# Weight and key preparation of three attentions as steps of the first batch, new step orders, and feed-forward scaling on VectorE

## The chip, the cores and the metric

The program runs on one core of one Trainium2 chip. The metric is the device time of one execution in microseconds (us). In the text PE is TensorE, DVE is VectorE, ACT is ScalarE, POOL is GpSimd and SP is SyncE, which here only issues DMAs. Each runs its own instruction stream in order; they meet through counting semaphores.

## The reference

Four layers work in turn on x (8 batches x 256 tokens x 128 features, fp32). Each layer is a gated cross-attention to a context (8 x 64 x 128) and a gated feed-forward:

```
x = x + tanh(g_xattn[l]) * attention_l(layernorm(x), ctx)
x = x + tanh(g_ffn[l])   * ffn_l(layernorm(x))          # l = 0..3
```

- Attention 0: 16 heads of 8 features; q = x Wq + bq; k, v = ctx Wkv + bkv; softmax; out Wo + bo.
- Attention 1: keys and values of the context and of x itself, no biases in q and k, a tanh gate in place of the first key's weight, and a layer norm of the result before the last projection.
- Attention 2: as attention 0 with a mask (8 x 1 x 256 x 64) that is scaled and added to the scores; scores divided by sqrt(128).
- Attention 3: 8 heads of 64 features.
- Feed-forward 0: 16 experts of 32 features, the best 4 of each token; 1: 8 experts of 352, the best 2; 2: one gated network of 384; 3: 8 experts of 64, the best 2 by groups, and a shared one.

## The kernel before

`build` (L2216) calls `setup`, then for each layer `attention` (L212; the last layer has `attention3`, L904) and `ffn` (L1234) or, for layers 0 and 3, `ffn_wide` (L1754). Nothing of two stages overlaps except some statistics. x stays in SBUF the whole time.

**A step table sets the order in an attention.** `STEPS_0` to `STEPS_3` list steps as (name, batch offset, group...). `passes(eng, does)` walks for v = -2 to 10 over the table, and for each row issues on engine `eng` that engine's part of the step, for batch v + offset. So all five engines have the same order of steps, each with its own part of them, and a row's place in the table decides what stands ahead of it on every engine. One walk over the table is one batch, here called a **cycle**.

A batch goes: "scale" (DVE L804, layer norm's scaling, with POOL in `turn` adding the gated output bias to x), "turn" (PE transposes L518, ACT and DVE split into a high and a low part, L686 and L810), "proj" (PE L535 to L537, ACT L698, DVE L823: q of one of 4 groups of 4 heads), "keys" (POOL L398 spreads the context's keys by head), "scores" (PE L551, in attention 2 also L553 with the mask, and DVE L835 takes row maxima), "maxima" (PE transposes L571, ACT, DVE L860), "weights" (PE scores again, transposed, less the maximum, ACT L711 exp), "pv" (PE L624), then the output is turned, divided, projected and added to x (`y`, DVE, semaphore x_done). In attention 2 "mask_in" (POOL L453) and "mask" (PE L526, ACT L692, DVE L817) prepare a batch's mask. `attention3` has steps of its own with the same walk.

**The prologue** of `attention` comes whole ahead of the table. DVE: 16 bn_aggr (L749); in layers 0 and 2 a wait for all of the layer's DMAs (`loaded`, in layer 2 also for the mask), then two copies of a bias row spread by head (L754, L756); the two weights split into high and low parts with spread columns, `wx` (L769, L770); PE turns the bias row into columns with 8 matmuls of one row (L481; the trace counts 16, each in two passes), DVE takes them (L773 to L775). PE: four key sums of three matmuls (L488 to L490), one for each group, into four PSUM banks; ACT L671 and DVE L785 take each in turn, through the one tile `hk`. PE: two value sums (L494, L496), ACT L674 takes them. DVE L792 copies a constant. POOL sets `mx`, `kc`, `vc` (L365 to L367), and scales `bo` (L385). Every engine's part ends with a wait for all of that, so that no PE instruction of batch 0 comes before it; DVE scales batch 0 (L804) only after its own last prologue instruction.

**`ffn_wide`**: four groups of 512 tokens. For each: statistics (DVE L2065, L2070), rstd (POOL L1895, L1897), scaling (group 0 on DVE, L2094; groups 1 to 3 on POOL, L1906), PE transposes (L1942), router logits (L1951). After the fourth, DVE routes all tokens at once (some 8 us up to `gx`, L2152), and PE spreads the gates (L1962). Meanwhile PE computes up-projections (L1972 to L1974, "up"): in layer 0 it has N = 16 of them ahead of the first gates. The scratch `gx` is zeroed by DVE (L2076) after the first group's statistics.

Of the kernel before, what the change touches and what calls it, by code (L numbers as in the profile page):

```python
# [113 lines left out]
def setup(pr):  # L114
# [60 lines left out]
    ("values", 0), ("scale", 1), ("scores", 0, 2, 0), ("proj", 0, 3), ("keys", 0, 3), ("maxima", 0, 1), ("weights", 0, 0, 0), ("pv", -1, 1, 0),  # L175
    ("turn", 1), ("scores", 0, 3, 0), ("proj", 1, 0), ("keys", 1, 0), ("maxima", 0, 2), ("weights", 0, 1, 0), ("spread", 0), ("o_turn", -1),
    ("o_norm", -1), ("scores", 1, 0, 0), ("proj", 1, 1), ("keys", 1, 1), ("maxima", 0, 3), ("weights", 0, 2, 0), ("pv", 0, 0, 0), ("o_scale", -1),
    ("on_turn", -1), ("scores", 1, 1, 0), ("proj", 1, 2), ("keys", 1, 2), ("maxima", 1, 0), ("weights", 0, 3, 0), ("y", -1),
# [3 lines left out]
    ("y", -2), ("weights", -1, 3, 3), ("keys", 0, 2), ("keys", 0, 3), ("weights", -1, 3, 4), ("scores", 0, 1, 4), ("scores", 0, 2, 0), ("scale", 1),  # L182
    ("proj", 0, 3), ("values", 0), ("maxima", 0, 1), ("pv", -1, 1, 0), ("weights", 0, 0, 0), ("pv", -1, 1, 1), ("keys", 1, 0), ("scores", 0, 2, 1),
    ("scores", 0, 2, 2), ("weights", 0, 0, 1), ("weights", 0, 0, 2), ("pv", -1, 1, 2), ("weights", 0, 0, 3), ("scores", 0, 2, 3),
    ("weights", 0, 0, 4), ("scores", 0, 2, 4), ("turn", 1), ("weights", 0, 1, 0), ("scores", 0, 3, 0), ("scores", 0, 3, 1), ("maxima", 0, 2),
    ("proj", 1, 0), ("spread", 0), ("pv", -1, 1, 3), ("pv", -1, 1, 4), ("scores", 0, 3, 2), ("weights", 0, 1, 1), ("weights", 0, 1, 2),
    ("scores", 0, 3, 3), ("scores", 0, 3, 4), ("o_turn", -1), ("weights", 0, 1, 3), ("weights", 0, 1, 4), ("o_norm", -1), ("scores", 1, 0, 0),
    ("proj", 1, 1), ("weights", 0, 2, 0), ("pv", 0, 0, 0), ("weights", 0, 2, 1), ("weights", 0, 2, 2), ("scores", 1, 0, 1), ("scores", 1, 0, 2),
    ("maxima", 0, 3), ("pv", 0, 0, 1), ("pv", 0, 0, 2), ("weights", 0, 2, 3), ("scores", 1, 0, 3), ("o_scale", -1), ("weights", 0, 2, 4),
# [2101 lines left out]
```

## Time and profile before

| | us |
|---|---|
| three runs | 1176.37, 1176.54, 1165.46 (median 1176.37) |
| profiled execution | 1168.41, its span 1166.6 |
| attention 0, 16.86 to 126.20 | 109.34 |
| feed-forward 0, to 193.60 | 67.40 |
| attention 1, to 442.70 | 249.10 |
| feed-forward 1, to 722.40 | 279.70 |
| attention 2, to 862.40 | 140.00 |
| feed-forward 2, to 922.60 | 60.20 |
| attention 3, to 1070.20 | 147.60 |
| feed-forward 3, to 1166.60 | 96.40 |

The stages' bounds are the first instruction of each stage in the timeline. The profiled execution spends 1.8 us outside its span. Busy shares of the whole span are 78% PE, 64% DVE, 48% ACT and 37% POOL; the mean granted clock of PE is 0.889 of full speed. A cycle is measured between the ends of `y` (x_done) of two batches.

### The profile page before, as it was taken

How to read it: one execution, taken by the hardware profiler on the slowest of the kernel's cores; microseconds unless marked ns; L12 is line 12 of the kernel's file. 1: busy time of each engine (PE TensorE's matmuls, PEld its weight loads, DVE VectorE, ACT ScalarE, POOL GpSimd, SP SyncE). 2: the span in 40 equal slices, each digit the busy share in tenths (PEclk: the TensorE clock that was granted, in tenths of full speed). 3: DMA queues.
4: the chain of work that ended last, by engine and by line, in shares of the span. 5: the costliest groups of instructions: out<-in, count | busy, mean ns of one | idle time of the engine just before them, and what ended most of it. 6: DMA issues, size and time to landing. Idle time of an engine off the chain costs nothing. (4 is left out here: it accounts for less than half of the span.)

```text
span 1166.6 us, 17099 instructions
## 1 busy us (share of the span) xinstructions
PE 912.0 (78%) x5366; PEld 686.6 (59%) x5366; DVE 746.8 (64%) x1823; ACT 563.8 (48%) x1091; POOL 428.7 (37%) x575
## 2 busy tenths in 40 slices
PE   2799586689899885888888885688858588885696
PEld 2677464556565643666666663477745357884574
DVE  3688467579998865757666564467756414555576
ACT  0477253367776762545555543256634233331364
POOL 2333414133443323655656565233310132220434
PEclk9799688689998995999999998689979769998699
DMA  4000000000001000000000001000000200000001
GB/s 129 1 2 2 1 0 22 1 20 20 19 21 37 20 2 0 1 1 1 1 1 1 1 1 23 16 2 1 2 21 1 72 1 1 1 1 1 0 1 37
DMA packets 25606, 14.12 MB, mean 12 GB/s; under 512 B 10775, under 2 KB 25006, under 8 KB 25390
## 3 DMA queue, kind: packets, MB, share of 16 engines
q1 hardware_dynamic: 25518, 13.03, 4.2%
q8 instruction: 45, 0.74, 0.3%
q14 instruction: 43, 0.35, 0.1%
HBM read 11.98 MB, written 1.05 MB: 11 GB/s over the span
## 5 line engine op out<-in xcount | busy, mean ns | idle before, releaser
L1433 POOL TENSOR_TENSOR L1f_h<-L1f_h,L1f_gb 128x512 f32<-128x512 f32 (+1 forms) x96 | 152.2, 1589 | 105.5 <-DVE L1f_h L1726 97.3
L711 ACT ACTIVATE L_pt<-bank 128x512 f32<-128x512 f32 x224 | 127.1, 597 | 44.0 <-PE bank L597 35.0
L398 POOL TENSOR_TENSOR L_kc<-L_kc_all,const 128x256 fp32r<-128x256 f32 x96 | 59.1, 618 | 177.8 <-PE bank L597 114.1
L698 ACT ACTIVATE L_part<-bank,L_bias_ca,const 128x256 fp32r<-128x256 f32 x128 | 68.9, 563 | 89.3 <-PE bank L537 88.8
L1562 ACT ACTIVATE L1f_a<-bank 128x512 f32<-128x512 f32 (+1 forms) x96 | 57.3, 597 | 112.7 <-PE bank L1487 112.6
L1726 DVE TENSOR_TENSOR L1f_h<-L1f_a,bank 128x512 f32<-128x512 f32 (+1 forms) x96 | 65.5, 682 | 70.8 <-ACT L1f_a L1562 70.3
L1734 DVE TENSOR_TENSOR L1f_h_lo<-L1f_h,L1f_h_hi 128x512 fp32r<-128x512 f32 (+1 forms) x96 | 88.2, 919 | 11.1 <-ACT L1f_h_hi L1575 11.1
L837 DVE TENSOR_REDUCE L_ms<-bank 128x2 f32<-128x512 f32 x128 | 84.0, 686 | 7.3 <-PE bank L558 7.2
L835 DVE TENSOR_REDUCE L_mc<-bank 128x8 f32<-128x512 f32 (+1 forms) x96 | 65.4, 682 | 19.5 <-PE bank L553 12.2
L1485 PE MATMUL bank<-L1f_xt_hi,big_hi 128*128 128x512 f32 (+1 forms) x192 | 77.8, 405 | 0.0
L1486 PE MATMUL bank<-L1f_xt_lo,big_hi 128*128 128x512 f32 (+1 forms) x192 | 76.8, 400 | 0.0
L1487 PE MATMUL bank<-L1f_xt_hi,big_lo 128*128 128x512 f32 (+1 forms) x192 | 76.7, 400 | 0.0
L558 PE MATMUL bank<-L_k,L_q 32*128 32x256 f32 x256 | 54.3, 335 | 16.6 <-DVE L_ms L837 15.1
L551 PE MATMUL bank<-L_kc,L_q 128*128 128x256 f32 x192 | 54.1, 345 | 15.8 <-DVE L_msk L817 6.4
L1507 PE MATMUL bank<-L1f_h_hi,big_hi 128*128 128x512 f32 (+1 forms) x96 | 41.4, 431 | 30.0 <-DVE L1f_h_lo L1734 29.7
L823 DVE SCALAR_TENSOR_TENSOR L_q<-bank,L_bias_c,L_part 128x256 fp32r<-128x256 f32 x96 | 46.2, 482 | 25.8 <-ACT L_part L698 23.6
L1575 ACT CAST L1f_h_hi<-L1f_h 128x512 fp32r<-128x512 f32 (+1 forms) x96 | 59.0, 615 | 2.1 <-POOL L1f_h L1433 2.1
L558 PEld LDWEIGHTS bank<-L_k,L_q 32*128 32x128 f32 x256 | 35.5, 199 | 32.9 <-DVE L_ms L837 21.3
L535 PE MATMUL bank<-L_xt_hi,L_wx 128*128 128x256 f32 x128 | 43.1, 337 | 9.9 <-DVE L_xt_lo L810 9.9
L551 PEld LDWEIGHTS bank<-L_kc,L_q 128*128 128x128 f32 x192 | 34.5, 208 | 27.6 <-issue 16.5
L705 ACT ACTIVATE L_hm<-bank,const 128x256 fp32r<-128x256 f32 x96 | 45.1, 470 | 6.3 <-PE bank L571 6.1
L1507 PEld LDWEIGHTS bank<-L1f_h_hi,big_hi 128*128 128x128 f32 (+1 forms) x96 | 17.9, 187 | 49.9 <-DVE L1f_h_lo L1734 44.8
(412 smaller groups left out, 2570.2 us busy)
## 6 DMA issues: line engine op xcount, KB each, us to landing
L_raw<-in_L_ffn_w_dram SPq DMA_DIRECT2D x8, 176.0 KB, 2.3
L_raw<-in_L_ffn_v_dram SPq DMA_DIRECT2D x8, 176.0 KB, 2.4
const<-in_const_dram SPq DMA_DIRECT2D x1, 1036.0 KB, 5.1
x<-in_x_dram SPq DMA_DIRECT2D x2, 512.0 KB
L_raw<-in_L_ffn_w_dram SPq DMA_DIRECT2D x8, 128.0 KB, 2.5
L_mask<-in_mask_Bx1xSxS_ff_dram SPq DMA_DIRECT2D x2, 512.0 KB
out_dram<-x SPq DMA_DIRECT2D x2, 512.0 KB
L_raw<-in_L_ffn_w_dram SPq DMA_DIRECT2D x8, 48.0 KB, 2.6
```

What stands on the lines that cost most here:

```text
L551: last = pe.matmul(o[:, t * S:(t + 1) * S], q[:, g, ts], kc[:, g], start=True, stop=not masked)
L558: last = pe.matmul(o[:, t * S:(t + 1) * S], q[rows, g, t * P:(t + 1) * P], k[rows, g], start=True, stop=True)
L698: last = act.activation(part[:, i].bitcast(F32R), b_proj[:, i * S:(i + 1) * S], ACT.Identity, bias=bias_ca[:, i, g:g + 1], scale=pr.c("ak" ...
L711: act.activation(pt[:, g // 2, (g % 2) * NS + (HEADS_1[i] if own_keys else i)], b_st[(g * NS + i) % 2][:], ACT.Exp, scale=scale).then_inc( ...
L835: dve.tensor_reduce(mc[:].rearrange("p t j -> p (t j)"), by_head[:, :, start:], AX_X, ALU.max).then_inc(sem["sc_taken"], 1)
L837: dve.tensor_reduce(ms[:, :, i - 1], bank.rearrange("p (t s) -> p t s", s=S), AX_X, ALU.max).then_inc(sem["sc_taken"], 1)
L1433: pool.tensor_tensor(h[0:m, r], h[0:m, r], gb[0:m, gate_slot(c)], ALU.mult).then_inc(sem["h_done"], 1)
L1485: pe.matmul(bank[0:m], hi[:, at:at + m], xh, start=True, stop=False)
L1486: pe.matmul(bank[0:m], hi[:, at:at + m], xl, start=False, stop=False)
L1487: last = pe.matmul(bank[0:m], lo[:, at:at + m], xh, start=False, stop=True)
L1726: dve.tensor_tensor(h[0:m, r], a[0:m, r], b_u[c % NS][0:m], ALU.mult).then_inc(sem["half_done"], 1)
L1734: dve.tensor_tensor(h_lo[0:m, r], h[0:m, r], h_hi[0:m, r].bitcast(F32), ALU.subtract).then_inc(sem["lo_done"], 1)
```

## The change

1. The prologue of `attention` becomes steps (`p_moments`, `p_bias`, `p_bias_c`, `p_wx`, `p_zero`, `p_kc`, `p_bo`, `p_const`, `p_vc`, and in layer 1 `p_wf`, `p_wx_zero`, `p_gate`, `p_vg`). A second table for each layer, `FIRST_0` to `FIRST_2`, orders them together with steps of batch 0; `passes` walks it once, ahead of the other table, and leaves those steps out later. The counting semaphores of the prologue and `loaded` are replaced by one for each thing that is waited for: the keys of group g wait for that group's sum, batch 0's values for the value sums, and so on. The key sums now use two banks in turn and the value sums one, since the others hold batch 0's work.
2. `p_moments 0` takes the two tiles of batch 0, `p_moments 1` the other 14, later.
3. The q and k biases come as rows of `bias_t` by 8 small DMAs, already spread, and one PE transpose makes them columns; the two copies and the 8 one-row matmuls go.
4. The mask of attention 2 gets its tile ahead of feed-forward 1, whose SP issues its two DMAs and waits for them.
5. All four step tables are new.
6. In `ffn_wide` DVE scales all four groups, POOL zeroes `gx` after the logits' first steps, the statistics come one group earlier in the order, and in layer 0 11 up-projections instead of 16 stand ahead of the gates.

```diff
 STEPS_2 = (
-    ("values", 0), ("scale", 1), ("mask_in", 1), ("scores", 0, 2, 0), ("proj", 0, 3), ("keys", 0, 3), ("maxima", 0, 1), ("weights", 0, 0, 0),
...
+    ("spread", 0), ("turn", 1), ("o_scale", -2), ("weights", 0, 0, 0), ("scores", 0, 3, 0), ("maxima", 0, 2), ("proj", 1, 0), ("o_norm", -1),
...
+FIRST_2 = (
+    ("p_bias",), ("p_const",), ("p_moments", 0), ("p_wx", 1), ("p_bias_c",), ("p_zero",), ("mask_in", 0), ("p_wx", 0), ("p_kc", 0), ("scale", 0),
+    ("mask", 0), ("keys", 0, 0), ("p_bo",), ("turn", 0), ("p_kc", 1), ("keys", 0, 1), ("proj", 0, 0), ("p_moments", 1), ("p_kc", 2), ("p_kc", 3),
+    ("scores", 0, 0, 0), ("proj", 0, 1), ("p_vc", 0), ("keys", 0, 2), ("keys", 0, 3), ("scores", 0, 1, 0), ("maxima", 0, 0), ("p_vc", 1),
+    ("proj", 0, 2),
+)
...
         def passes(eng, does):
+            for step, *at in first:
+                if step in does:
+                    does[step](*at)
             for v in range(-2, B + 3):
                 for step, db, *at in table:
-                    if step in does and 0 <= v + db < B:
+                    if step in does and 0 <= v + db < B and (step, v + db, *at) not in first:
                         does[step](v + db, *at)
...
+                    for i, (name, row) in enumerate({0: (("L0_xattn_bq", 0), ("L0_xattn_bkv", 0)), 2: (("L2_xattn_bq", 0), ("L2_xattn_bk", 0))}[layer]):
+                        for t in range(4):
+                            sp.dma_start(bias_t[NG * i:NG * i + NG].rearrange("g (h t d) -> g h t d", h=GH, t=4)[:, :, t],
+                                         ins[name][0:D].rearrange("(g h d) -> g h d", g=NG, h=GH)).then_inc(sem["bias_dma"], 16)
...
+                def p_bias():
+                    if biased:
+                        pe.wait_ge(sem["bias_dma"], 16 * 8)
+                        pe.transpose(b_sc[1][:, 0:2 * NG], bias_t[:], pr.id(2 * NG)).then_inc(sem["bias_turned"], 1)
...
+                def p_kc(g):
+                    if g == 0:
+                        pe.wait_ge(sem["wx_ready"], 2)
+                    need(pe, sem["kc_split"], g - 1)
                     cols = slice(g * P, (g + 1) * P)
+                    bank = b_st[g % 2]
...
                 def keys(b, g):
                     need(pool, sem["st_done"], b * U + (g + 1) * NS - U)
+                    if b == 0:
+                        pool.wait_ge(sem["kc_split"], g + 1)
...
-        AHEAD = N if layer == 0 else 6
-        first = [("moments", 0), ("scale", 0), ("moments", 1), ("turn", 0), ("scale", 1), ("logits", 0), ("moments", 2), ("turn", 1), ("scale", 2),
-                 ("up", 0), ("logits", 1), ("moments", 3), ("turn", 2), ("scale", 3), ("up", 1), ("logits", 2), ("turn", 3), ("logits", 3),
-                 ("route", 0)] + [("up", n) for n in range(2, AHEAD)]
+        AHEAD = 11 if layer == 0 else 6
+        first = [("moments", 0), ("prepare", 0), ("moments", 1), ("scale", 0), ("moments", 2), ("scale", 1), ("turn", 0), ("logits", 0), ("moments", 3),
+                 ("turn", 1), ("zero", 0), ("scale", 2), ("up", 0), ("logits", 1), ("turn", 2), ("scale", 3), ("up", 1), ("logits", 2),
+                 ("turn", 3), ("logits", 3), ("route", 0)] + [("up", n) for n in range(2, AHEAD)]
...
                 def scale(i):
-                    if i:
-                        return
-                    dve.wait_ge(sem["rstd"], 1)
+                    dve.wait_ge(sem["rstd"], i + 1)
+                    need(dve, sem["xn_turned"], i - 1)
```

**The start of attention 2 on PE, before.** Names: `ctx_hi`, `ctx_lo` the context's parts, `wx` the weights' parts, `xn` the scaled x, `mk` a mask tile.

```order
L481 MATMUL bank<-L_ones,L_bias_x 128x1 x8
L488 MATMUL bank<-ctx_hi,L_wx 128x512
L489 MATMUL bank<-ctx_lo,L_wx 128x512
L490 MATMUL bank<-ctx_hi,L_wx 128x512
...
L494 MATMUL bank<-L_bias_row,L_ones 128x512
L496 MATMUL bank<-w_att,ctx_t 128x128 x4
L494 MATMUL bank<-L_bias_row,L_ones 128x512
L496 MATMUL bank<-w_att,ctx_t 128x128 x4
L518 MATMUL bank<-const,L_xn 128x128 x2
L535 MATMUL bank<-L_xt_hi,L_wx 128x256
L536 MATMUL bank<-L_xt_lo,L_wx 128x256
L537 MATMUL bank<-L_xt_hi,L_wx 128x256
```

And now (lines 516 to 518 are the key sums, 551 the transposes of x, 570 to 572 the projection, 588 and 590 the scores):

```order
L508 MATMUL bank<-const,L_bias_t 128x8
L516 MATMUL bank<-ctx_hi,L_wx 128x512
L517 MATMUL bank<-ctx_lo,L_wx 128x512
L518 MATMUL bank<-ctx_hi,L_wx 128x512
L559 MATMUL bank<-const,L_mk 128x128 x2
L551 MATMUL bank<-const,L_xn 128x128 x2
L516 MATMUL bank<-ctx_hi,L_wx 128x512
L517 MATMUL bank<-ctx_lo,L_wx 128x512
L518 MATMUL bank<-ctx_hi,L_wx 128x512
L570 MATMUL bank<-L_xt_hi,L_wx 128x256
L571 MATMUL bank<-L_xt_lo,L_wx 128x256
L572 MATMUL bank<-L_xt_hi,L_wx 128x256
```

The turn and the first projection of batch 0 stood behind all four key sums and both value sums; now they stand behind two key sums, and the value sums (L526, L530) behind the first scores.

**A steady cycle of attention 2 on PE, before**, from the second half of one batch's "weights" (L588, L590, L591) on:

```order
L588 MATMUL bank<-L_q,L_kc 128x256
L590 MATMUL bank<-L_msk_all,L_i 128x256
L591 MATMUL bank<-L_mt,L_selc 128x256
L526 MATMUL bank<-const,L_mk 128x128 x2
L641 MATMUL bank<-const,L_ot 128x128 x4
L551 MATMUL bank<-L_kc,L_q 128x256
L553 MATMUL bank<-L_i,L_msk 128x256
```

And now ("weights" are L628, L630, L631):

```order
L683 MATMUL bank<-const,L_ot 128x128 x4
L559 MATMUL bank<-const,L_mk 128x128 x2
L570 MATMUL bank<-L_xt_hi,L_wx 128x256
L571 MATMUL bank<-L_xt_lo,L_wx 128x256
L572 MATMUL bank<-L_xt_hi,L_wx 128x256
L628 MATMUL bank<-L_q,L_kc 128x256
L630 MATMUL bank<-L_msk_all,L_i 128x256
L631 MATMUL bank<-L_mt,L_selc 128x256
L628 MATMUL bank<-L_q,L_kc 128x256
L630 MATMUL bank<-L_msk_all,L_i 128x256
L631 MATMUL bank<-L_mt,L_selc 128x256
L588 MATMUL bank<-L_kc,L_q 128x256
```

Between the mask's transposes and the next batch's first scores, which need the mask through ACT and DVE, stood one operation of four transposes; now a projection and a whole "weights" step stand there.

**The start of feed-forward 3 on DVE, before** (`mv` the statistics, `xt_lo` the low part of the transposed tile):

```order
L2065 BN_STATS st<-x 128x6 x4
L2070 BN_AGGR L3f_mv<-st 128x2 x4
L2076 MEMSET L3f_gx 128x2048
...
L2094 TENSOR_SCALAR L3f_xn<-x,L3f_mv,L3f_rstd 128x128 x4
L2065 BN_STATS st<-x 128x6 x4
L2070 BN_AGGR L3f_mv<-st 128x2 x4
L2099 TENSOR_TENSOR L3f_xt_lo<-bank,L3f_xt_hi 128x512
```

And now:

```order
L2117 BN_STATS st<-x 128x6 x4
L2122 BN_AGGR L3f_mv<-st 128x2 x4
L2143 TENSOR_SCALAR L3f_xn<-x,L3f_mv,L3f_rstd 128x128 x4
L2117 BN_STATS st<-x 128x6 x4
L2122 BN_AGGR L3f_mv<-st 128x2 x4
L2143 TENSOR_SCALAR L3f_xn<-x,L3f_mv,L3f_rstd 128x128 x4
L2148 TENSOR_TENSOR L3f_xt_lo<-bank,L3f_xt_hi 128x512
```

The zeroing of `gx` is gone from DVE, and the second group is scaled there before the first group's transposed tile is split.

## Rows read from the trace of the kernel before

**Rows 1.** The page, busy time, its share of the span, and instructions.
```profile
PE 912.0 (78%) x5366; PEld 686.6 (59%) x5366; DVE 746.8 (64%) x1823; ACT 563.8 (48%) x1091; POOL 428.7 (37%) x575
```

**Rows 2.** Windows, attentions 0 to 3: us; busy per engine; PE clock, DMA.
```profile
16.86:126.20 109.34, 90.40 (x624) 70.77 (x624) 77.36 (x207) 60.21 (x134) 39.67 (x68) 0.92 0.03 7
193.60:442.70 249.10, 209.13 (x1712) 141.29 (x1712) 199.85 (x455) 155.28 (x314) 86.11 (x183) 0.89 0.07 19
722.40:862.40 140.00, 106.44 (x768) 87.58 (x768) 81.86 (x217) 68.75 (x143) 41.65 (x80) 0.85 0.05 9
922.60:1070.20 147.60, 119.72 (x664) 98.70 (x664) 58.17 (x117) 44.44 (x85) 37.97 (x64) 0.89 0.06 15
```

**Rows 3.** Timeline, prologue of attention 0: start, us, instruction, [idle before <- releaser].
```profile
17.78 0.36 SPq L331 DMA_DIRECT2D L_bo<-in_L_xattn_bo_dram  x1
21.12 0.41 DVE L754 COPY L_bias_x<-L_bias_row 1x512 f32<-1x512 f32 x1 [2.93 <-DMA L_bo<-in_L_xattn_bo_dram]
22.35 3.57 PE L481 MATMUL bank<-L_ones,L_bias_x 1*128 1x1 f32 x16 [14.57 <-DVE L_bias_x L756]
26.79 0.79 PE L488 MATMUL bank<-ctx_hi,L_wx 128*128 128x512 f32 x1 [0.86 <-DVE L_bias_ca L775]
34.53 0.75 DVE L785 SCALAR_TENSOR_TENSOR L_kc_all<-bank,L_bias_c,L_q 128x512 fp32r<-128x512 f32 x1 [0.97 <-ACT L_q L671]
34.74 1.16 PE L496 MATMUL bank<-w_att,ctx_t 128*128 128x128 f32 x8
40.13 0.80 PE L551 MATMUL bank<-L_kc,L_q 128*128 128x256 f32 x2 [1.18 <-DVE L_q L823]
```

**Rows 4.** Timeline, start of attention 2.
```profile
732.41 0.41 DVE L754 COPY L_bias_x<-L_bias_row 1x512 f32<-1x512 f32 x1 [7.88 <-DMA L_mask<-in_mask_Bx1xSxS_ff_dram]
752.60 0.55 PE L551 MATMUL bank<-L_kc,L_q 128*128 128x256 f32 x1 [1.17 <-DVE L_msk L817]
```

**Rows 5.** Timeline, the first reduction of attention 1.
```profile
216.42 0.68 DVE L835 TENSOR_REDUCE L_mc<-bank 128x8 f32<-128x504 f32 x1 [0.89 <-PE bank L551]
```

**Rows 6.** Windows, single cycles: attentions 0, 2, 3, 1; then the first of attention 2.
```profile
86.23:95.75 9.52, 8.89 (x74) 7.02 (x73) 8.31 (x23) 6.84 (x16) 3.67 (x7) 1.00 0.00 0
811.65:824.22 12.57, 10.78 (x93) 9.08 (x92) 8.99 (x25) 7.89 (x17) 4.43 (x9) 1.00 0.01 1
1021.97:1035.77 13.80, 12.28 (x82) 10.92 (x81) 6.88 (x12) 4.47 (x9) 3.35 (x7) 1.00 0.00 0
281.65:307.13 25.48, 22.70 (x210) 14.96 (x211) 24.31 (x55) 18.65 (x38) 9.86 (x21) 1.00 0.08 22
758.84:773.50 14.66, 12.58 (x73) 11.03 (x74) 8.01 (x22) 8.26 (x16) 4.15 (x9) 0.69 0.00 1
```

**Rows 7.** Waits in attention 2, 765 to 848: us in total, times, longest.
```profile
PE bank L551 <- DVE L_msk L817: 5.2, 7, 1.1
PE bank L526 <- DVE L_mt L860: 4.0, 6, 0.7
```

**Rows 8.** Waits in attention 3, 985 to 1065: us in total, times, longest.
```profile
PE bank L1073 <- ACT L_rb L1157: 3.9, 6, 0.7
```

**Rows 9.** Timeline, start of feed-forward 0.
```profile
128.98 1.76 DVE L2076 MEMSET L0f_gx<- 128x2048 f32 x1 [0.38 <-issue]
139.26 1.11 PE L1942 MATMUL bank<-const,L0f_xn 128*128 128x128 f32 x4 [2.18 <-POOL L0f_xn L1906]
145.10 3.13 POOL L1906 TENSOR_SCALAR L0f_xn<-x,L0f_mv,L0f_rstd 128x128 f32<-128x128 f32 x4
160.68 0.69 DVE L2152 TENSOR_TENSOR L0f_gx<-L0f_p,L0f_total 128x512 f32<-128x512 f32 x1
163.89 0.60 PE L1962 MATMUL bank<-const,L0f_gx 128*128 128x128 f32 x4
```

**Rows 10.** Lines, POOL's `kc` memset and DVE's scaling in attentions: ns min/median/max.
```profile
L366 POOL MEMSET L_kc<- x3: 952/952/1562, 22.0 to 728.1; 128x1024 f32 x3
L804 DVE TENSOR_SCALAR L_xn<-x,L_mv,L_rstd x48: 334/340/504, 35.6 to 837.1; 128x128 f32<-128x128 f32 x48
```

More of the change, by code:

```diff
@@ L174 @@
 STEPS_0 = (
[L175 to L178, printed above, removed]
+    ("keys", 0, 0), ("o_scale", -2), ("weights", -1, 3, 0), ("scores", 0, 2, 0), ("turn", 1), ("maxima", 0, 1), ("weights", 0, 0, 0),
@@ L179 @@
 )
 STEPS_1 = (
[L182 to L189, printed above, removed]
@@ L190 @@
-    ("scores", 1, 0, 4), ("proj", 1, 2), ("keys", 1, 1), ("on_turn", -1), ("scores", 1, 1, 0), ("maxima", 1, 0), ("weights", 0, 3, 0),
-    ("pv", 0, 0, 3), ("pv", 0, 0, 4), ("scores", 1, 1, 1), ("weights", 0, 3, 1), ("weights", 0, 3, 2), ("scores", 1, 1, 2), ("scores", 1, 1, 3),
+    ("y", -2), ("weights", -1, 3, 3), ("weights", -1, 3, 4), ("scores", 0, 1, 4), ("scores", 0, 2, 0), ("scale", 1), ("proj", 0, 3), ("values", 0),
+    ("maxima", 0, 1), ("weights", 0, 0, 0), ("scores", 0, 2, 1), ("scores", 0, 2, 2), ("pv", -1, 1, 0), ("pv", -1, 1, 1), ("weights", 0, 0, 1),
@@ new lines @@
+FIRST_1 = (
+    ("p_wf",), ("p_bias",), ("p_moments", 0), ("p_bias_c",), ("p_wx_zero",), ("p_wx", 1), ("p_zero",), ("p_wx", 0), ("p_kc", 0), ("scale", 0),
+    ("keys", 0, 0), ("p_bo",), ("turn", 0), ("p_kc", 1), ("proj", 0, 0), ("keys", 0, 1), ("p_gate",), ("p_const",), ("p_moments", 1), ("p_kc", 2),
+    ("scores", 0, 0, 0), ("scores", 0, 0, 1), ("scores", 0, 0, 2), ("p_kc", 3), ("proj", 0, 1), ("keys", 0, 2), ("keys", 0, 3), ("scores", 0, 0, 3),
+    ("scores", 0, 0, 4), ("p_vc", 0), ("p_vc", 1), ("maxima", 0, 0), ("p_vg", 0), ("p_vg", 1),
@@ L654, in y @@
                     last.then_inc(sem["y_done"], 1)
[L656 removed]
+                passes(pe, {"p_wf": p_wf, "p_bias": p_bias, "p_kc": p_kc, "p_vc": p_vc, "p_vg": p_vg, "turn": turn, "mask": mask, "proj": proj, "scores": scores, "maxima": maxima, "weights": weights,
                             "values": values, "pv": pv, "o_turn": o_turn, "on_turn": on_turn, "y": y})
@@ L759, in _, with p_moments @@
-                if gated:
-                    prep(dve.memset(wx[:].rearrange("p w (h t d) -> p (w h) t d", t=4, d=HD)[:, :, 3].bitcast(F32), 0.0))
-                    dve.wait_ge(sem["prep_act"], 1)
-                for i in range(2):
+                def p_moments(k):
+                    tiles_of = (range(2), range(2, NT))[k]
+                    for tile in tiles_of:
+                        last = dve.bn_aggr(mv[:, tile], pr.st6[:, tile])
+                    last.then_inc(sem["moments"], 1)
```

373 lines of the change are left out of this document (198 added, 175 removed).

## The prediction

> **What bounds the kernel now.** The page comes first: PE is busy for 78% of the span, DVE for 64% [rows 1]. An average over stages says nothing of any one of them, so the windows by stage come next. In the attentions PE is busy for 76 to 84% of its time, and DVE for 80% in attention 1 alone, 39 to 71% elsewhere [rows 2]. PE thus leaves 19, 40, 34 and 28 us idle in attentions 0 to 3. The third view splits them: the timeline shows where each prologue ends, the single cycles what a batch costs. The fourth, the waits, names what PE misses in a cycle.
>
> **Attention 0, prologue.** DVE sits until 21.12 for the last bias transfer; PE's one-row matmuls take 3.57 us from 22.35, and the key sums start 0.9 us after them, at 26.79; DVE takes the fourth at 34.53; the value sums follow on PE, 2.3 us each, half of it the 1.16 of L496; and batch 0's first scores come at 40.13 [rows 3]. From 34.53 + 0.75 to 40.13, 4.9 us, goes the chain scale, turn, projection, which needs nothing of the last three sums. With the change:
> - The splits of `wx` start at about 18.3 and need no bias. The 8 bias transfers take SP about 8 x 0.35 us from 16.86 (0.36 for one issue), so the last is issued at 19.3, and lands 3.3 us later as `bo` did (21.12 - 17.78), at 22.7. One transpose instead of 3.57 us: sums start at about 23, 3.8 earlier.
> - The first scores need one key sum (its share of 26.79 to 35.3 is 2.1 us for each of four), POOL's keys, and the chain of 4.9, which runs beside the sums. One sum, the chain and 1.5 to 2 us for standing behind two sums on PE, ACT and DVE: 23 + 2.1 + 4.9 + 2 = 32. Gain 8.1.
> - Given back: two value sums (2 x 2.3, less what falls into PE's pauses, I take 2.6) and two ACT and DVE parts of sums in batch 0's path, 0.7: 3.3. The 14 bn_aggr, 1.0 us, lie under PE's sums. Net **-4.7**. Bounds: -8.1 (all fits into pauses) and 0 (all is in batch 0's way; the bank swap makes the sums take turns).
>
> **Attention 2, prologue.** The wait is for the mask, until 732.41, and first scores come at 752.60 [rows 4], 20.2 us later (19.0 in attention 0). The mask is now loaded a stage earlier. Stage start 722.40 to bias landed is 6 to 7 us, and 9 to 10 more as above, with slower matmuls at the start: 739.7. Gain 12.9, 3.3 given back: **-9.6**, bounds -13 and -3 (the wait alone, part of it).
>
> **Attention 1, prologue.** There are no bias transfers; the first reduction is at 216.42 [rows 5]. The same chain (turn to reduction) moves beside sums 2 to 4: to about 209.5, -6.9. The value sums and the gate's sums give back some 1.4: **-5.5**, bounds -7 and 0. The three sum to -19.8.
>
> **Cycles.** Each full-clock cycle [rows 6] against what PE is busy in it:
> - Attention 2: 12.57 with 10.78 busy. Over 83 us (6.6 cycles) PE waits 5.2 us for the mask's last split ahead of the scores and 4.0 us for the subtraction ahead of the mask's transposes [rows 7], 1.4 a cycle. The new order puts a projection and a "weights" step between the mask's transposes and the scores that need it, and other steps behind the maxima. Both waits vanish; others show up for a part. PE busy is modelled, so the floor may lie somewhat lower. I take 11.0: 7 cycles x -1.5 = **-10.5**; bounds 0 and -1.8 x 7.
> - Attention 3: 13.80 with 12.28 busy; 0.65 of the 1.5 idle is the wait for the reciprocals ahead of the first projection of values [rows 8]. The divisions now open the next walk. I take 12.8: 7 x -1.0 = **-7**; bounds 0 and -10.5.
> - Attention 0: 9.52 with 8.89 PE and 8.31 DVE; there is little left: 9.1, 7 x -0.4 = **-2.8**.
> - Attention 1: DVE is busy for 24.31 of 25.48. Its work is the same, so the new order gives at most 1.1 a cycle; I take **0**.
>
> **Feed-forwards 0 and 3.** POOL takes 3.13 us for a group's scaling and paces groups 1 to 3; PE waits 2.18 us before the second turn [rows 9]. The same op on DVE is 0.34 us a tile [rows 10], 1.4 a group, and DVE loses the 1.76 us memset: 1.76 + 3.13 - 1.4 = 3.5 us sooner at the second group. From there PE's own steps are the pace, and I take -3.2 at the fourth in layer 0. Gates: `gx` is ready at 161.37 but PE reaches them at 163.89, behind its queue of up-projections [rows 9]. With 11 ahead they start 2.5 us sooner, but 5 are then done later, in places where PE is mostly the limit: -1.3 net. In layer 3 the groups were already nearer to PE's pace: -2.5. Sum **-7**; bounds -2 and -11.
>
> A place to be careful: the scaling on DVE. The one `kc` memset on POOL that ran beside DVE's copies took 1562 ns, the others 952, and DVE's own scaling between 334 and 504 [rows 10]. So the two slow one another; at the worst 24 scalings by 0.16 us, 3.8 us, mostly under PE. I leave it at nothing in the sum. The Trainium skill ("GPSIMD Engine Reference", section 1, Specifications) says that VectorE and GpSimd contend for SBUF ports they share in some modes; that speaks for moving less onto DVE while POOL works. By it alone the feed-forwards would give about 3 us rather than 7, and the total would be 1125.
>
> **Sum.** -19.8 (prologues) - 20.3 (cycles) - 7 (feed-forwards) = -47. The profiled execution took 1168.4, 1.8 outside the span; 1168.4 - 47 = **1121 us**. The median of the runs shown, 1176.4, lies 8 above it, but one of three was at 1165.5, so both levels are seen, and the profiled one is what the terms were read in. Measured against the median the change would be -4.7%.
>
> **Rivals.**
> - *The cycles stay.* The cycle is a chain through five engines for one batch, not a sum of PE's waits: a wait removed in one place comes back in the next, since the steps of a batch feed one another through single tiles (`hk`, `q`, one bank each). For it: in attention 0 PE is at 8.89 of 9.52 and attention 1's DVE at 24.31 of 25.48, orders which an earlier table already filled [rows 6]. Against: PE busy at 86% of the cycle and each wait has a name. Then prologues -12 (more of them is given back too) and feed-forwards -7: 1149. Chance 0.17.
> - *PE's clock stays high.* Attention 2's first cycle took 14.66 against 12.57, at a clock of 0.69 [rows 6]: 2.1 us for a clock that fell to 1.2 GHz in the prologue's pauses. If the new start keeps PE at 2.4 GHz through them, four attentions give 2.1 us more each: 1121 - 8.5 = 1112. For it: PE's pauses in the prologue become shorter. Against: PE still has nothing to do until the first transfers land (it idles 14.57 us there now [rows 3]), and so the fall stays. Chance 0.18. The Trainium skill ("TensorE: Matmul & The Clock Gate", Part 1) says that PE's clock follows its recent activity, and that rule is what would make this one come out.
> - *No change.* Cycles stay, and the prologue's work costs as much in batch 0 as it did before: only the -7 is left: 1161, -0.6%. Chance 0.07.
> - *Slower.* The low clock holds in steady cycles. New orders that wait longer at one point (a "weights" step queued ahead of a "scores" step stalls PE for both when its maxima are late) give one long pause a cycle instead of three short ones, and PE falls to the level of the first cycles: +2.1 a cycle in 24 cycles, +50, with prologues and feed-forwards -27 and no gain in the cycles: 1191. It decides from 13 of 24 cycles on. Against: PE kept 1.00 with waits of up to 1.1 us [rows 6, 7]. Chance 0.05.
>
> The forecast itself has 0.53. The range takes it in with the clock's rival below and most of the first above, and the bounds of the prologues (0 to -28) and cycles (0 to -34) reach no further with any weight: **1104 to 1150**. What a measurement of this kernel tells from no change is about 1%, 12 us. Faster: 0.53 + 0.17 + 0.18 = 0.88; the same 0.07; slower 0.05.
>
> **What would show it.** Step by step in the profile of the changed kernel: first scores of attention 0 at 32, of attention 2 some 17 us after its start (30 before), the reduction of attention 1 some 16 after (22.8 before); cycles of 11.0, 12.8, 9.1 and 25.5; no wait of scores for the mask; feed-forward 0 near 63 us and 3 near 94. Wrong would be: a cycle in attention 2 above 12.3, a new wait of a key sum for the bank before it that delays batch 0 as long as the prologue did, or a granted clock under 0.9 in the steady cycles.

## The result and the profile after

| | before | changed |
|---|---|---|
| runs, us | 1176.37, 1176.54, 1165.46, 1171.85 (median 1174.11) | 1095.08, 1107.10, 1102.93, 1099.87 (median 1101.4) |
| profiled execution, its span | 1168.41, 1166.6 | 1095.08, 1093.3 |
| mean granted clock | 0.889 | 0.913 |

The ratio is 0.9388, with a 95% interval of 0.9354 to 0.9422: 6.1% faster. Forecast were 1121 us (1104 to 1150); the direction is right, the gain is 73 us where 47 were forecast, and the median lies 3 us below the range.

Where the 73 us are is read by stage. Each stage is measured here from the start of the last x update of the stage before (DVE's SCALAR_TENSOR_TENSOR into x) to the start of its own last one, and attention 0 from 16.86 us, so the parts add up to the span but for these 16.9 us ahead and the tail of 7.1 us behind, the same in both. The third column is a kernel of the experiments below: the changed one with the four old step tables.

| stage | before | old tables | changed | gain | forecast |
|---|---|---|---|---|---|
| attention 0 | 108.8 | 105.8 | 100.4 | -8.4 | -7.5 |
| feed-forward 0 | 66.2 | 63.2 | 61.8 | -4.4 | -4.5 |
| attention 1 | 250.4 | 260.7 | 242.4 | -8.0 | -5.5 |
| feed-forward 1 | 278.4 | 276.4 | 278.3 | -0.1 | 0 |
| attention 2 | 141.3 | 129.9 | 112.2 | **-29.0** | -20.1 |
| feed-forward 2 | 59.0 | 59.2 | 59.3 | +0.3 | 0 |
| attention 3 | 148.9 | 148.7 | 129.7 | **-19.2** | -7 |
| feed-forward 3 | 89.8 | 86.2 | 85.4 | -4.4 | -2.5 |

Attentions 2 and 3 hold 21 of the 26 us by which the forecast was too small. The windows of single cycles of the changed kernel, in the order of attentions 0, 2, 3, 1 (us; busy us and instructions of PE, PEld, DVE, ACT, POOL; granted clock, DMA share, GB/s), answer to [rows 6]:

```profile
78.43:87.28 8.85, 8.53 (x74) 6.96 (x73) 8.54 (x23) 7.09 (x17) 3.62 (x7) 1.00 0.01 2
777.81:788.10 10.29, 10.29 (x92) 8.98 (x91) 9.12 (x23) 7.91 (x18) 4.34 (x10) 1.00 0.01 3
963.20:974.77 11.57, 11.57 (x83) 10.90 (x81) 6.55 (x13) 4.68 (x9) 3.38 (x7) 1.00 0.00 1
266.41:291.11 24.70, 23.05 (x212) 15.60 (x210) 23.52 (x55) 18.43 (x38) 9.83 (x21) 1.00 0.08 23
```

In attentions 2 and 3 PE is busy without a gap, 10.29 of 10.29 and 11.57 of 11.57. And the busy time itself fell, from 10.78 and 12.28, with the same matmuls. Rows of attention 3 before show how:

```profile
1022.25 0.28 PE L1045 MATMUL bank<-L_xt_lo,L_wq_hi 128*128 128x256 f32 x1
1022.37 0.28 PE L1046 MATMUL bank<-L_xt_hi,L_wq_lo 128*128 128x256 f32 x1
1023.38 2.05 PE L1057 MATMUL bank<-L_kb,L_q 128*128 128x128 f32 x16 [0.73 <-ACT L_q L1137]
...
1026.43 0.44 PE L1064 MATMUL bank<-const,L_mx 128*128 128x128 f32 x2
...
1028.00 0.67 PE L1073 MATMUL bank<-L_q,L_kb 128*128 128x256 f32 x2 [0.66 <-ACT L_rb L1157]
```

A record lasts 0.28 us, but in a row the next one starts 0.12 us later and the records overlap. Ahead of a pause nothing overlaps the last record, so 0.16 us more of it counts as busy. So a busy share is no floor: a part of it is pauses too. The Trainium skill says of a lone matmul ("TensorE: Matmul & The Clock Gate", "Step-by-step: what each phase is for") that the drain of one overlaps the fill of the next, so that only an isolated one pays it, and the trace agrees: 0.7 us of busy time went with the pauses.

Read from start to start, the pauses of this cycle add up to the whole difference. From the start of the last matmul ahead of each to the start of the second one behind it, they cost 0.99 us (at L1057), 0.35 (at L1064, 0.13 idle) and 0.89 (at L1073) more than the same steps take in a row: 2.23, and the cycle fell from 13.80 to 11.57.

The waits in the same cycle of attention 3 (us in total, times, longest) begin with these. None is a wait of PE, where [rows 8] had one:

```profile
POOL L_vb L1066 <- PE bank L1150: 6.8, 1, 6.8
DVE L_rs L1266 <- PE bank L1139: 4.5, 1, 4.5
ACT L_hr L1210 <- DVE L_rs L1266: 3.7, 1, 3.7
```

The starts, from the timeline. Rows that answer to [rows 3] (attention 0: an issue of biases on SP, the bias transpose, the first scores), [rows 4] (attention 2, the same three) and [rows 5]:

```profile
20.89 1.28 SPq L346 DMA_DIRECT2D L_bias_t<-in_L_xattn_bkv_dram  x2
23.57 0.27 PE L508 MATMUL bank<-const,L_bias_t 8*128 8x8 f32 x1 [16.02 <-DMA L_bias_t<-in_L_xattn_bkv_dram]
32.60 0.41 PE L588 MATMUL bank<-L_kc,L_q 128*128 128x256 f32 x2
...
196.90 0.67 DVE L890 TENSOR_REDUCE L_mc<-bank 128x8 f32<-128x504 f32 x1
...
705.00 2.63 SPq L346 DMA_DIRECT2D L_bias_t<-in_L_xattn_bk_dram  x4
708.84 0.27 PE L508 MATMUL bank<-const,L_bias_t 8*128 8x8 f32 x1 [9.26 <-DMA L_bias_t<-in_L_xattn_bk_dram]
717.92 0.41 PE L588 MATMUL bank<-L_kc,L_q 128*128 128x256 f32 x1
```

First scores come 7.5 us sooner in attention 0 (8.1 forecast), 13.8 in attention 2 counted from the stage's start (12.9), and attention 1's first reduction 6.7 (6.9). One issue of a bias DMA took 0.66 us (2.63 for four), not the 0.35 assumed, and PE's transpose started at 23.57.

In feed-forward 0, PE meets the gates with a wait where [rows 9] had them behind its queue. They start 13.7 us sooner in the program and 5.3 within the stage:

```profile
149.45 0.69 DVE L2202 TENSOR_TENSOR L0f_gx<-L0f_p,L0f_total 128x512 f32<-128x512 f32 x1
150.20 0.65 PE L2014 MATMUL bank<-const,L0f_gx 128*128 128x128 f32 x4 [1.27 <-DVE L0f_gx L2202]
```

DVE and POOL do slow one another here. DVE's scaling of the third group runs beside POOL's zeroing of `gx` and takes 1.59 us, against 1.08 to 1.11 for the other three (one tile took 1020 ns, the median is 341). It is the same in feed-forward 3, 0.5 us in each:

```profile
130.54 1.80 POOL L1962 MEMSET L0f_gx<- 128x2048 f32 x1
131.40 1.59 DVE L2143 TENSOR_SCALAR L0f_xn<-x,L0f_mv,L0f_rstd 128x128 f32<-128x128 f32 x4
...
L2143 DVE TENSOR_SCALAR L0f_xn<-x,L0f_mv,L0f_rstd x16: 315/341/1020, 123.8 to 136.7; 128x128 f32<-128x128 f32 x16
```

The starts of stages also depend on the granted clock, and it differs from execution to execution. These are the starts of attention 3 up to batch 0's update of x, first in the changed kernel, then in earlier_turn below, which has the same code and the same 193 matmuls there:

```profile
871.15:928.50 57.35, 39.91 (x193) 29.51 (x193) 19.99 (x53) 18.16 (x32) 20.07 (x27) 0.85 0.14 37
...
875.74:935.93 60.19, 44.40 (x193) 33.30 (x193) 18.95 (x54) 18.22 (x32) 20.09 (x27) 0.74 0.13 36
```

At 0.74 against 0.85 PE is busy for 4.5 us more and the start is 2.8 us longer. A difference of 2 or 3 us between two starts of stages is therefore read as an order's only where the clocks are alike. The full cycles of attentions 2 and 3 ran at 1.00 in every profile.

### The profile page after: what moved, and what is told of

Read it like the earlier page. It is cut to its first block and busy times, and to the rows that moved or that the text cites. A ratio compares the mean times of both kernels' runs of the same rounds, so it can differ in the third digit from the quotient of the medians.

```text
span 1093.3 us, 17068 instructions
## 1 busy us (share of the span) xinstructions
PE 879.5 (80%) x5336; PEld 666.8 (61%) x5336; DVE 746.9 (68%) x1844; ACT 565.1 (52%) x1091; POOL 414.0 (38%) x559
## 3 DMA queue, kind: packets, MB, share of 16 engines
HBM read 11.99 MB, written 1.05 MB: 12 GB/s over the span
## 5 line engine op out<-in xcount | busy, mean ns | idle before, releaser
L588 PE MATMUL bank<-L_kc,L_q 128*128 128x256 f32 x192 | 48.6, 316 | 5.8 <-DVE L_ms L892 2.3
L570 PE MATMUL bank<-L_xt_hi,L_wx 128*128 128x256 f32 x128 | 43.9, 343 | 3.9 <-DVE L_q L878 2.3
L637 PE MATMUL bank<-L_mt,L_k 32*128 32x256 f32 x256 | 43.7, 337 | 3.0 <-ACT L_pt L762 2.2
```

## The experiments

All are edits of the changed kernel unless it is said otherwise. Since the stages follow one another, one kernel can hold an edit in each of several stages, and each is read in its own windows. Where a ratio to the kernel before is given, the interval is 95%. "First" is the time from a stage's start to batch 0's update of x. The runs probe_new, probe_old, one_move, move_divide, two_moves and prepared_late were executed once; they are read by their full cycles, which repeat within 0.05 us in attentions 2 and 3 (but for two cycles of prepared_late).

**old_orders.** The prologue steps without the new tables.

```diff
-STEPS_0 .. STEPS_3 of the changed kernel
+STEPS_0 .. STEPS_3 of the kernel before
```

> The changed kernel with the four step tables of before; the prologue steps (FIRST tables) and the feed-forwards stay as changed. Theory A (PE paced with pauses): in attentions 2 and 3 a cycle was PE's work plus pauses, and the new tables take out all pauses and the matmul tails that each pause exposes. Then the old tables bring back cycles of 12.6 and 13.8 us (10.3 and 11.6 now), 9.5 in attention 0 and about 25.5 in attention 1, and attention 3 is again about 149 us long (129.7 now). In the whole about 40 us over the changed kernel's 1095, near 1135. Theory B (the orders were worth what was forecast, 20 us, and the rest came from the prologue steps and the clock): cycles at 12.6 and 13.8 only in part, total near 1116.

Measured: 1133, 1140, 1148 and 1156 us; the ratio, 0.972 (0.964 to 0.980), leaves out the longest, which is the profiled one. Cycles are 9.53, 12.57 and 13.81 us in attentions 0, 2 and 3, the old ones within 0.01; the stages stand in the table above. The cycles of attentions 2 and 3 here:

```profile
802.23:814.81 12.58, 10.78 (x91) 9.09 (x91) 8.98 (x24) 7.88 (x18) 4.42 (x10) 1.00 0.00 0
999.01:1012.82 13.81, 12.28 (x82) 10.93 (x81) 6.89 (x12) 4.47 (x9) 3.34 (x7) 1.00 0.00 1
```

This is theory A. Attention 3 is 19.0 us longer with the old table, nearly its whole gain. Of these, 16.9 come after batch 0, at a clock of 1.00 but for the last batch (0.90 with the old table); the 2.1 in batch 0 (59.5 against 57.4, at clocks of 0.74 and 0.85) can as well be the clock. In attention 2 the table is worth 17.7 and the new prologue 11.4. Of the 17.7, five full cycles give 11.4 and batch 0, which runs through the same table, 6.9 (54.2 to 47.3, at clocks of 0.81 and 0.80); the last two batches give back 0.6. In attention 0 the two are 5.4 and 3.0 in this pair, but batch 0 took 43.3 to 46.9 us in the four kernels with the old table here and this prologue, and 43.9 to 45.2 in three with the new one. There the table is worth 2.4 us after batch 0, and its part in batch 0 isn't resolved. Attention 1 can't be read from this pair: four of its cycles ran at a granted clock of 0.87 here, and its last two batches at 0.73 and 0.64.

**serial_first.** The new tables without the overlap.

```diff
-    ("p_bias",), ("p_moments", 0), ("p_wx", 1), ..., ("p_kc", 0), ("scale", 0), ("keys", 0, 0), ("p_bo",), ("turn", 0), ...
+    all ("p_...") steps in their order, then ("scale", 0), ("keys", 0, 0), ("turn", 0), ...
```

> The changed kernel with each FIRST table sorted: all prologue steps first, in their order, then the steps of batch 0. The finer waits, the columns by DMA, the early mask and the new step tables stay. Theory A (the overlap of the prologue with batch 0 is what shortens the start): the end of batch 0 comes 5 us later in attentions 0, 1 and 2, total +15, 1110. Theory B (the start was shortened by what was taken out of it, the one-row matmuls and the waits for late transfers): under 1.5 us each, total under +5.

Measured: 1119.0 us, ratio 0.956 (0.949 to 0.962). First: attention 0 43.9 to 50.9, attention 2 47.3 to 56.5, attention 1 87.4 to 97.0; the cycles stay at 8.86, 10.30 and 11.57. Theory A, and more than its 5 us a stage. A part of the last two is the clock, which fell from 0.80 to 0.70 and from 0.77 to 0.68 in these starts; in attention 0 it was 1.00, so the 7.0 us are the order's. Without the overlap attention 0 would be where it was (49.9 before).

**loads_and_gates.** Three undoings in three stages.

```diff
+ attention 2: sp.dma_start(mask2[:, :, h], ...) x2 behind the biases; POOL waits for both before mask_in 0
-AHEAD = 11 if layer == 0 else 6
+AHEAD = N if layer == 0 else 6
+ feed-forward 3: pool.tensor_scalar(xn, ...) for groups 1 to 3
```

> Three parts of the change undone in three stages that do not touch one another. Attention 2: the mask's two DMAs are issued by SP in this stage again, behind the biases. Feed-forward 0: 16 up-projections ahead of the gates again, not 11. Feed-forward 3: groups 1 to 3 scaled by POOL again. Expected: attention 2's start longer by 3 to 5 us if the mask's arrival again is what batch 0 waits for, by under 1 if the key sums hide it. Feed-forward 0 longer by 1.3 us (forecast) or unchanged if PE is the limit anyway. Feed-forward 3 longer by 2 us if POOL's scaling paces the groups, under 0.5 if PE does.

Measured: 1115.9 us, ratio 0.943 (0.936 to 0.949). Attention 2's first went from 47.3 to 51.5, +4.2, at a clock of 0.80 in both: the mask's arrival is what batch 0 would wait for, and PE's row shows it:

```profile
734.09 0.69 PE L564 MATMUL bank<-const,L_mk 128*128 128x128 f32 x2 [5.86 <-POOL L_mk L490]
```

In feed-forward 3 the fourth turn comes 15.2 us after the first (15.3 in the kernel before), where DVE scales 11.5 to 13.1: POOL's scaling was the pace. The stage took 88.7 us, against 85.4 to 87.6 where DVE scales, so 1.1 to 3.3 us of it reach the stage's end. In feed-forward 0 the gates came 1.4 us later on PE (34.4 against 33.0 after the stage's start), and the stage took 62.3 us. With 11 ahead it took 61.8 in nine kernels and 63.2 in two, so 16 against 11 is worth 0.5 at most, not the 1.3 forecast.

**warm_pe.** Filler work for the clock.

```diff
+                        for _ in range(16):
+                            pe.matmul(b_o[:], pr.ctx_hi[:, 0:P], pr.ctx_hi[:], start=True, stop=True)
                         pe.wait_ge(sem["bias_dma"], 16 * 8)
```

> The changed kernel with matmuls on PE whose result nobody reads, put where PE has nothing to do at the start of a stage: 16 (512 columns, fp32r) in attentions 0, 2 and 3, 6 in attention 1 behind its weights' transposes, 12 in each feed-forward. They add work to keep PE's clock from falling. If the low clock at the stages' starts is worth what attention 2's first cycle showed, 2.1 us a stage, eight stages give about -12 to -17 us, 1080, and the granted clock of the starts rises to 0.95. If the start is a chain through DVE, ACT and transfers in which the clock matters little, the change is within 3 us.

Measured: 1102.1 us, ratio 0.940 (0.932 to 0.947), the changed kernel's own. First 42.6, 87.6, 47.6, 58.1 in the four attentions, against 43.9, 87.4, 47.3, 57.4, at clocks of 0.88, 0.77, 0.86, 0.81 against 0.92, 0.77, 0.80, 0.85. Among the attentions the filler raised the clock in attention 2 alone, and there gave no time. In feed-forward 2 it did: the clock of the start rose from 0.70 to 0.85, the nine transposes that open it on PE took 1.14 us instead of 2.15, and its first update of x came after 29.8 us instead of 31.7 (31.0 to 32.0 in all other kernels with the change). In feed-forward 0 the first turn came 1.7 us later than without filler and the stage took 63.5 us. So the gains and losses cancel; that a higher clock is worth nothing is not shown.

**probe_new and probe_old.** A known amount of work more on PE in each batch.

```diff
                     need(pe, sem["xt_lo"], b)
+                    for _ in range(8):
+                        pe.matmul(b_turn[:, 0:S], wx[:, 0, 0:P], pr.ctx_hi[:, 0:S], start=True, stop=True)
                     for t in range(2):
```

> The changed kernel with 8 matmuls more in each batch's turn on PE in all four attentions (128x128 by 256 columns, fp32r, result not read): some 0.12 us each from start to start, 0.94 us a batch. Theory A (PE has no pause left in attentions 2 and 3, so it alone sets the cycle): their cycles grow by the whole 0.94, to 11.2 and 12.5 us. In attention 1, where VectorE is the busiest, by under 0.3. Theory B (a chain of steps through all engines sets the cycle, PE happens to be busy beside it): under 0.4 in attentions 2 and 3 too.

> The same 8 matmuls a batch with the step tables of before. Where PE pauses 1.4 to 1.5 us in a cycle and the pauses are slack, a part is taken up by them: under 0.5 us more on 12.57 and 13.80. If the cycle of before was a chain that runs through the turn, all 0.94 comes on top, and the pauses stay as long as they were.

Cycles of attentions 2 and 3 and, third, of attention 1 in probe_new:

```profile
793.45:804.74 11.29, 11.29 (x100) 9.97 (x99) 9.13 (x24) 7.94 (x18) 4.34 (x10) 1.00 0.01 1
985.38:997.89 12.51, 12.51 (x91) 11.88 (x89) 6.54 (x12) 4.68 (x9) 3.39 (x7) 1.00 0.01 1
...
278.11:303.77 25.66, 24.00 (x220) 16.58 (x218) 23.53 (x55) 18.55 (x38) 9.83 (x21) 1.00 0.08 23
```

and of attentions 2 and 3 in probe_old:

```profile
824.16:837.73 13.57, 11.81 (x99) 10.06 (x99) 8.98 (x25) 7.92 (x18) 4.42 (x10) 1.00 0.01 1
1026.03:1040.80 14.77, 13.24 (x90) 11.89 (x89) 6.88 (x13) 4.58 (x9) 3.35 (x7) 1.00 0.00 0
```

With the new tables +0.98 and +0.94: PE alone sets the cycle, as theory A has it. With the old ones +1.00 and +0.96 as well, and the idle time stays (1.76 and 1.53 us): the pauses were no slack. Each began when PE had handed a result to ACT or DVE and had to have it back for its very next step, so added work elsewhere in the cycle went on top. Of probe_old's two cases the second came, all of it on top; under 0.5 had been expected if the pauses were slack. In attention 1 the expectation of under 0.3 failed: it took all of it (24.70 to 25.66), and PE's idle time stayed there too (1.65 and 1.66). DVE's 23.5 of 24.7 busy did not make it the engine that sets attention 1's pace.

**one_move.** Old tables, one move each in attentions 2 and 3.

```diff
 STEPS_2: ("spread", 0), ("mask", 1), ("o_turn", -1), ("o_norm", -1),
-    ("scores", 1, 0, 0), ("proj", 1, 1), ("keys", 1, 1), ("maxima", 0, 3), ("weights", 0, 2, 0),
+    ("proj", 1, 1), ("weights", 0, 2, 0), ("scores", 1, 0, 0), ("keys", 1, 1), ("maxima", 0, 3),
 STEPS_3:
+    ("divide", -1, 0), ("divide", -1, 1), ("values", 0), ("scale", 1), ... ("maxima", 1),
-    ("values", 0), ("scale", 1), ... ("maxima", 1), ("divide", 0, 0), ("divide", 0, 1),
```

> The step tables of before with one move each in attentions 2 and 3 (attentions 0 and 1: the old tables). Attention 3: the two divide steps go from the end of the walk to the head of the next. Attention 2: one projection and one weights step are put between a batch's mask and the next scores. Theory A (each pause of PE costs its idle time and the tail of the matmul before it that then shows, together about 1.1 us, and pauses go one by one): each move takes one pause out, 12.8 and 11.5 us a cycle. Theory B (a wait removed comes back at the next place, the first rival of the prediction): cycles unchanged, 13.8 and 12.6.

Attention 2's cycle fell to 11.65, attention 3's stayed:

```profile
777.67:789.32 11.65, 10.53 (x91) 9.01 (x91) 8.84 (x24) 8.06 (x18) 4.38 (x10) 1.00 0.00 0
```

0.92 for one pause (its 0.7 idle, and 0.25 less busy). Attention 3's move was badly chosen: the divides stay next to the weights in PE's order, so nothing changed there, and PE still waits 0.7 us for the copy of the reciprocals. Opening the next walk with the divisions is what the prediction named as the remedy in attention 3; by itself it is worth nothing.

**move_divide and two_moves.** Moves that do change PE's order.

```diff
 STEPS_3 (both):      ("scores", 1, 1), ("divide", 0, 0), ("pv", 0, 1), ("maxima", 1), ("divide", 0, 1)
 STEPS_2 (both):      as one_move, and ("o_turn", -1) ahead of ("mask", 1)
 STEPS_3 (two_moves): ("y", -1) behind ("proj", 1, 1), ("keys", 1, 1)
 STEPS_2 (two_moves): ("turn", 1) ahead of ("weights", 0, 0, 0)
```

> The run one_move moved attention 3's divides past nothing that PE does, so its order of PE work was the old one. Here, with the step tables of before elsewhere, the first divide goes ahead of the second value product, so that PE has that product and the maxima between a divide and the weights that wait for its copy. In attention 2 the move of one_move, and the mask's transposes behind the output's. If pauses go one by one: attention 3's cycle 12.8 us (13.8 before), the wait of the weights for ACT's copy gone; attention 2's 11.2 to 11.4 (11.66 with one move). If a removed wait comes back elsewhere: 13.8 and 11.66.

> As move_divide, and one more move in each. Attention 3: y goes behind the second projection, between it and the scores that wait for ACT's copy of q. Attention 2: the next batch's turn goes ahead of a weights step instead of standing right before the projection. If PE's pauses were all that the old orders cost, attention 3's cycle is 11.6 to 11.8 and attention 2's 10.4 to 10.7, the same as with the whole new tables (11.57 and 10.30). If the new tables did something else as well, a gap of over 0.5 us stays.

Attention 2: 11.51, then 11.01, where 11.2 to 11.4 and 10.4 to 10.7 were expected. Attention 3: 13.73, then 13.79, no gain, where 12.8 and 11.6 to 11.8 were expected. PE's waits in one cycle of attention 3, first in move_divide, then in two_moves:

```profile
PE bank L1131 <- DVE L_mt L1261: 0.8, 1, 0.8
PE bank L1115 <- ACT L_q L1195: 0.7, 1, 0.7
```

```profile
PE bank L1102 <- ACT L_q L1195: 0.8, 1, 0.8
PE bank L1131 <- DVE L_mt L1261: 0.8, 1, 0.8
```

Before, they were the copy of the reciprocals (L1073) and q ahead of the scores (L1057). The first move took out the wait for the copy, and the weights (L1131) then waited for the maxima, which now had one divide behind them instead of two. The second put y between the projection and the scores, and of the two halves of the projection, now side by side, the second (L1102) waited for ACT to take the first. Two pairs of neighbours that depend on one another went, two others came. That is the prediction's first rival, and in attention 3 it holds for single moves; the whole new table is where it does not.

**prepared_late.** PE's order exactly that of the changed kernel in attention 3; only DVE's and POOL's preparation is placed otherwise.

```diff
-    ("scale", 2), ("values", 1), ("keys", 2, 0), ("keys", 2, 1)
+    ("scale", 1), ("values", 0) at the head, ("keys", 1, 0), ("keys", 1, 1) ahead of the scores
```

> The changed kernel with attention 3's table altered so that PE's order is word for word that of the changed kernel, but scaling, keys and values are prepared in the walk that uses them, as before the change, and not one walk ahead: 'scale 1' and 'values 0' at the head, 'keys 1' right ahead of the scores. If PE's own order (no two steps of PE that depend on one another side by side) is what made the cycle 11.57, it stays under 11.9. If the look-ahead of POOL's and VectorE's preparation is as much a part of it, PE waits for xn and kb and the cycle grows by 0.7 to 1.1 for each, to 12.3 or more (13.8 with the old table).

```profile
959.10:971.72 12.62, 11.79 (x83) 10.81 (x81) 6.95 (x12) 4.68 (x9) 3.38 (x7) 1.00 0.01 1
```

```profile
PE bank L1093 <- DVE L_xn L1239: 0.8, 1, 0.8
```

So the look-ahead of a whole walk is worth 1.05 us on top of PE's order, from 12.62 to 11.57: without it the turn waits for its own batch's scaling. The rest, from 13.80 to 12.62, goes to PE's order. What the look-ahead would give with the old order wasn't run.

**bias_in_two.** Two bias transfers instead of eight.

```diff
-                        for t in range(4):
-                            sp.dma_start(bias_t[...][:, :, t], ins[name][0:D].rearrange(...))
+                        sp.dma_start(bias_t[...], ins[name][0:D].rearrange(...).unsqueeze(2).to_broadcast([NG, GH, 4, HD]))
```

> The changed kernel with the q and k biases brought in by 2 DMAs instead of 8, the four copies of each read from the same source by a step of zero. In the changed kernel SP took 5.4 us to issue the eight in attention 2 and PE started at 708.84, 9.3 us after its last instruction. If the issues hold up the start, PE starts 3 us sooner in attentions 0 and 2 and batch 0 ends 2.5 us sooner in each: -5 in all, 1.5% faster at most not reached. If the transfer with 512 small pieces takes as long as eight short ones, under 1 us.

Measured: median 1095.6 us of 6, ratio 0.935 (0.930 to 0.940), an interval that overlaps the changed kernel's (0.935 to 0.942). The starts show it more clearly: PE began 3.4 us sooner in attention 2 (5.8 us after the stage's start instead of 9.2) and at 19.77 instead of 23.57 in attention 0. First fell from 43.9 to 41.4 in attention 0 and from 47.3 to 43.9 in attention 2, 5.9 us in all, as expected.

**earlier_turn.** That, and batch 0's scaling and turn ahead of the first key sum, in all three FIRST tables; on PE the biases' transpose comes behind that sum.

```diff
 FIRST_0:
-    ..., ("p_wx", 1), ("p_bias_c",), ("p_zero",), ("p_wx", 0), ("p_kc", 0), ("scale", 0), ("keys", 0, 0), ("p_bo",), ("turn", 0), ...
+    ..., ("p_wx", 1), ("p_zero",), ("scale", 0), ("p_wx", 0), ("turn", 0), ("p_bias_c",), ("p_kc", 0), ("keys", 0, 0), ("p_bo",), ...
```

> The changed kernel with the biases in two transfers, and new FIRST tables: batch 0's scaling and turn ahead of the first key sum instead of behind it (on POOL the addition of the gated bias stays behind the first keys), and on PE the biases' transpose behind the first key sum instead of ahead of it. bias_in_two ends batch 0 at 41.4 and 43.9 us after the start of attentions 0 and 2. If the start is a chain of transfer, key sum, turn and projection, each stage's batch 0 ends 1.5 to 3 us sooner than that, attention 1's 1 us sooner, total 1088. If the two key sums behind it on ACT and VectorE are what decides, under 0.5 a stage.

Measured: median 1092.6 us of 6, ratio 0.930 (0.926 to 0.933), the fastest kernel here, and clear of the changed one (0.935 to 0.942). From bias_in_two alone it isn't clear. First in attention 0 is 39.9, 1.4 less, just under the 1.5 to 3 expected. In attention 2 it was 48.6 in its profile, 4.7 more, at a clock of 0.75 against 0.83, and in attention 1 87.8 where the changed kernel has 87.4, so the gain in these two stays open.

## Why the prediction was right in sign and short in size

Split at batch 0's update of x, the 73.3 us between the two profiles are 29.1 up to it in the four attentions, 35.5 behind it, and 8.7 in the feed-forwards. Forecast were 19.8 (prologues), 20.3 (cycles) and 7.

- **The prologues** were forecast at -19.8. First scores, or the first reduction, came within 0.9 us of the forecast in all three. With the old tables, the ends of batch 0 in old_orders give -3.0, -2.1 and -11.4 in attentions 0, 1 and 2, where -4.7, -5.5 and -9.6 were forecast: -16.5, near enough in the sum. The single values vary with the execution: the four kernels with the old tables there give -3.0 to -6.6 in attention 0 and -2.1 to -3.9 in attention 1. So attention 0 is right, attention 1 gave back more in batch 0 than was allowed for, and attention 2 gave more than forecast. The early mask is 4.2 us of the -11.4.
- **The feed-forwards**, forecast -7, gave -8.8 in the two profiles; by the spread of the other kernels' stages (61.8 to 63.2 and 85.4 to 87.6) it is -5 to -9. Right within that. The contention of DVE and POOL, left at nothing in the sum, is there where POOL zeroes `gx`, 0.5 us in each of the two.
- **The cycles** are the step that failed: "I take 11.0", "I take 12.8", "9.1", in all -20.3, and 0 in attention 1. Measured: 10.30, 11.57 and 8.86, and 24.70 instead of 25.47 in attention 1. Behind batch 0 that is -10.8, -16.8, -2.4 and -5.6 us in attentions 2, 3, 0 and 1. The worst term is attention 3's, -7 against -16.8. Attention 2's batch 0, which runs through the same table, adds -6.9 that no term had.
- **What was wrong in it.** A removed pause was priced at its idle time, and one of 0.7 us costs 0.9 to 1.0 from start to start. "Others show up for a part" was an allowance for what did not happen: PE has no wait left. In attention 3 the prediction took one wait of 0.65 and put it "ahead of the first projection of values"; L1073 is the "weights" step, and a second wait as long stood ahead of the scores, for q. Opening the walk with the divisions did nothing alone (one_move); what brought 11.57 was an order with no dependent neighbours (12.62) and preparation a walk ahead (prepared_late).
- **A part was luck.** The term "7 cycles x -1.5" in attention 2 came out as -10.8, but as five full cycles of -2.27, less 0.6 given back by the last two batches, which never ran full cycles. In attention 3 the last two gave 5.6 (20.1 to 14.5).
- The bounds "0 to -1.8 x 7" of attention 2 and "-10.5" of attention 3 were made from PE's busy time as a floor, and the range was argued from them ("cycles (0 to -34)"). The terms behind batch 0 alone came to -35.5. With 11.57 as the floor, attention 3's bound would have been -15.6 for seven cycles.
- In attention 1 DVE was taken for the bound, by its busy share. probe_new shows that it isn't.
- **Rivals.** *The cycles stay*: its mechanism is real (move_divide, two_moves), but a table written so that no two neighbours on PE depend on one another escapes it. *PE's clock stays high*: this came in part and is not excluded as a share of the gain. The clocks of the four starts were 0.83, 0.77, 0.69 and 0.74 before and 0.92, 0.77, 0.80 and 0.85 in the changed kernel's profile; in attention 3 such a difference goes with 2.8 us, and with the same code attention 1's start took 87.4 us at 0.77 and 93.5 at 0.71. It can't explain the full cycles, at 1.00 before and after in attentions 2 and 3. *No change* and *slower*: PE stayed at 1.00 in the cycles of attentions 2 and 3.

## What to carry to other kernels

Where one engine works through a fixed order, as PE does here, count the pairs of neighbouring steps in which the second needs what other engines make of the first. The cycle is the engine's steps in a row plus one pause for each pair. Price a pause from start to start (0.9 to 1.0 us here), not by its idle time (0.7), and look for an order with none; in attention 3 single moves only made another pair. Ask too whether the other engines prepare a batch early enough (1.05 us here). Added work that comes in full on top does not prove an engine saturated: look at whether its idle time is zero.
